# DLRM tower on one core: late transposes and partial sums behind a round of sums, inner products on four quarters of the array

## The reference, cut to what matters

```
e = stack([tbl_f[ids[:, f]] for f in range(40)], axis=1)      # (512, 40, 64)
i, j = np.triu_indices(40, k=1)                               # 780 pairs
z[b, p] = sum_de  e[b, i_p, d] * W[p, d, e'] * e[b, j_p, e']  # (512, 780)
h = relu(concatenate([z, dense_ctx], 1) @ W_top1 + b_top1)    # (512, 796) @ (796, 512)
h = relu(h @ W_top2 + b_top2)                                 # @ (512, 256)
y = h @ W_top3                                                # @ (256, 1)
```

## Time and profile before

| | |
|---|---|
| median of 3 runs | 380.26 us (380.23 to 380.48) |
| the profiled execution, its own time | 379.78 us |
| its span, first to last instruction | 378.0 us |
| PE busy | 348.8 us, 92% |
| DVE busy | 277.1 us, 73% |
| POOL busy | 171.0 us, 45% |
| ACT busy | 45.4 us, 12% |
| mean granted clock of PE | 0.982 of full |

### The profile page before, as it was taken

One profiled execution on the slowest core, in us unless ns is written; L12 is line 12 of the kernel. 1 busy time (PEld: TensorE's weight loads), 2 busy tenths in 40 slices (PEclk: granted clock), 3 DMA queues, 4 the chain that ended last, 5 costly groups with the idle time before them and its releaser, 6 DMA issues.

```text
span 378.0 us, 4628 instructions
## 1 busy us (share of the span) xinstructions
PE 348.8 (92%) x1784; PEld 125.0 (33%) x1784; DVE 277.1 (73%) x287; ACT 45.4 (12%) x73; POOL 171.0 (45%) x261
## 2 busy tenths in 40 slices
PE   0864886899999999999999999999999999999997
PEld 0532332433333333333333333333333333333342
DVE  3999998569687777866758877796778788878420
ACT  2112310111010030101010120000000000300142
POOL 6888888506788775544535553252344100000000
PEclk9978898999999999999999999999999999999999
DMA  5355632012162421121122112220221000000000
GB/s 186 90 167 163 180 125 62 14 57 69 30 264 76 134 74 28 58 69 33 46 71 69 45 37 66 69 69 10 65 68 59 10 2 0 2 1 0 2 0 0
DMA packets 11448, 24.29 MB, mean 64 GB/s; under 512 B 3857, under 2 KB 3857, under 8 KB 11298
## 3 DMA queue, kind: packets, MB, share of 16 engines
q1 hardware_dynamic: 7330, 19.79, 15.6%
q0 software_dynamic: 4096, 4.20, 5.4%
HBM read 23.98 MB, written 0.00 MB: 63 GB/s over the span
## 4 chain that ended last, share of the span: by engine, by line
PE 86%; DVE 9%; DMA 2%; ACT 1%; issue 1%; SPq 0%
PE y_ps L491 46%; PE z_ps L515 24%; DVE one_hot L392 7%; PE t_ps L470 4%; PE y_ps L523 3%; PE t_ps L446 3%; PE t_ps L461 2%; DMA table<-in_small_tables 2%; PE y_ps L498 2%; PE y_ps L553 2%; DVE x L401 1%; DVE table_parts L386 1%; DVE prod L422 1%; PE t_ps L559 0%; ACT x L326 0%
## 5 line engine op out<-in xcount | busy, mean ns | idle before, releaser
L422 DVE TENSOR_TENSOR prod<-y_ps,x 128x1024 f32<-128x1024 f32 x190 | 220.8, 1218 | 61.6 <-PE y_ps L491 58.6
L491 PE MATMUL y_ps<-x,w_sb 64*128 64x512 f32 x760 | 185.5, 617 | 12.1 <-DVE prod L422 5.1
L302 POOL DMA_INDIRECT rows<-in_tbl,ids_sb x128 | 126.0, 984 | 124.0 <-PE y_ps L491 92.7
L491 PEld LDWEIGHTS y_ps<-x,w_sb 64*128 64x128 f32 x760 | 67.1, 188 | 117.2 <-issue 59.1
L515 PE MATMUL z_ps<-prod,selector 128*32 128x512 f32 x780 | 94.3, 598 | 0.0
L297 POOL MEMSET spacer<- 128x256 f32 x127 | 44.3, 349 | 0.2
L515 PEld LDWEIGHTS z_ps<-prod,selector 128*32 128x32 f32 x780 | 20.4, 109 | 67.0 <-issue 36.3
L392 DVE TENSOR_SCALAR one_hot<-ids_all,numbers 128x512 fp32r<-128x512 int32 x64 | 34.4, 607 | 0.0
L446 PE MATMUL t_ps<-one_hot,table_parts 128*128 128x512 f32 x56 | 18.6, 479 | 14.0 <-DVE one_hot L392 9.7
L328 ACT ACTIVATE x<-t_ps 128x512 f32<-128x512 f32 x15 | 9.0, 599 | 156.4 <-PE t_ps L461 151.4
L446 PEld LDWEIGHTS t_ps<-one_hot,table_parts 128*128 128x128 f32 x56 | 11.9, 226 | 21.6 <-issue 12.7
(11 more groups left out here) (36 smaller groups left out, 59.8 us busy)
## 6 DMA issues: line engine op xcount, KB each, us to landing
w_sb<-in_w_units SPq DMA_DIRECT2D x25, 512.0 KB
ids_all<-in_ids_one_hot SPq DMA_DIRECT2D x8, 256.0 KB
table<-in_small_tables SPq DMA_DIRECT2D x8, 256.0 KB
rows<-in_tbl,ids_sb POOLq DMA_INDIRECT x128
w_sb<-in_w SPq DMA_DIRECT2D x1, 1792.0 KB
w_sb<-in_w SPq DMA_DIRECT2D x1, 512.0 KB
ids_sb<-in_ids SPq DMA_DIRECT2D x1, 80.0 KB, 2.0
z_sb<-in_dense_t SPq DMA_DIRECT2D x1, 32.0 KB
```

What stands on the lines that cost most here:

```text
L302: pool.indirect_dma_start(rows[:, n % ROW_SLOTS, bt, h * D:(h + 1) * D], None, tables[f], bass.IndirectOffsetOnAxis(ap=ids_sb[:, bt, f:f + ...
L422: dve.tensor_tensor(prod[:, at:at + 2, :], y_ps[:, s % Y_SLOTS], leaf, ALU.mult).then_inc(prod_ready, 1)
L491: ins = pe.matmul(y_ps[:, slot, h, :], w_sb[own, c % W_SLOTS, at:at + P], x[own, m, :], start=True, stop=True)
```

## The change

Three things are edited. In `plan_jobs`, the turn of every pair from k = 7 on is moved to the nearest earlier place behind a round of sums, 0 to 3 units earlier. The partial sums of the first layer are put 8 units apart in place of 6, so that all of them stand behind a round. And the inner units are laid out anew: before, the two fields' matmuls went from rows 0 to 63 into partitions 64 to 127 and from rows 64 to 127 into partitions 0 to 63, two on each of two quarters of the array; now the four matmuls go to four different quarters. The weights, the copies of the "mix" job and the rows of `W_top1` are laid out to match. The rows are split between banks so that bank 0 gets low to low and high to high, and bank 1 gets low to high and high to low.

```diff
-PARTIAL_EVERY = 6
+PARTIAL_EVERY = 8
@@ pairs_of
-    return [(1 - n % 2, n // 2, n % 2, 2 * (a + n) + 1 - n % 2, 2 * (a + n) + n % 2) for n in range(4)]
+    return [(n % 2, n // 2, n % 2 ^ n // 2, 2 * (a + n) + n % 2, 2 * (a + n) + 1 - n % 2) for n in range(4)]
@@ plan_jobs
         at = FIRST[k] - LEADS.get(k, LEAD)
+        if k > max(ONE_HOT_PAIRS):
+
+            at -= (at - SUM_LAG - ROUND) % ROUND
@@ ACT, mix
-                    k, own = 4 * q + n, slice(D * (n % 2), D * (n % 2) + D)
+
+                    k, into, other = 4 * q + n, D * (n % 2 ^ n // 2), D * (1 - n % 2)
                     wait_x(act, k)
-                    act.activation(x_mix[own, q % MIX_SLOTS, n // 2, :], x[own, k, :],
+                    act.activation(x_mix[into:into + D, q % MIX_SLOTS, n // 2, :], x[other:other + D, k, :],
                                    ACT.Copy).then_inc(mixed, 1)
@@ PE, multiply, inner unit
-                for own, into, first in ((low, high, 1), (high, low, 0)):
-                    for bank in range(2):
-                        k = 4 * unit[1] + 2 * bank + first
-                        ins = pe.matmul(y_ps[into, slot, bank, :],
-                                        w_sb[own, c % W_SLOTS, at + D * bank:at + D * bank + D], x[own, k, :],
-                                        start=True, stop=True)
+                for bank in range(2):
+                    for h, own in enumerate((low, high)):
+                        ins = pe.matmul(y_ps[(low, high)[h ^ bank], slot, bank, :],
+                                        w_sb[own, c % W_SLOTS, at + D * bank:at + D * bank + D],
+                                        x[own, 4 * unit[1] + 2 * bank + h, :], start=True, stop=True)
```

## The result

The changed kernel takes 375.86 us (median of 4 runs, 375.31 to 376.20) against 380.28 us for the kernel before in the same runs: ratio 0.9879, 95% interval 0.9864 to 0.9894. That is 4.4 us less, and 0.3 us above the forecast of 375.6 us. The profiled execution took 376.20 us, the slowest of the four, with a span of 374.4 us.

What follows compares the result with a forecast made beforehand. PE was taken to bound the kernel from 75 to 354 us, DVE keeping pace. -2.73 - 3.44 + 1.52 = -4.65 us, giving 375.6 us, range 374.7 to 377.4.

Steps and rivals of the forecast that it cites:

- 13 cuts: Past 75 us, moved turns and partial sums no longer cut pieces of units: 13 times 0.21, 2.73 us less.
- 4 inner units: Units 28, 63, 114 and 181 on four quarters take two steps, not four: 0.86 us each, 3.44 us less.
- 2 waits for ACT: At units 135 and 151 a partial sum waits for ACT's copy of the turn: 0.76 us each, 1.52 more.
- The first inner unit: At 50.05 us, off the bound stretch: its gain is nothing, since PE then waits 3.94 us for DVE anyway.
- The mix copies: ACT's copies in the mix job: new partitions cost nothing, and even a copy twice as long would stay hidden.
- The Trainium skill's rule against it: Different row tiles can't work on one PSUM bank together: inner units would stay at four steps, bringing 0.
- The lower bound: Turn and partial sum share shape 128*128, so perhaps 0.20 us for changing shape goes: each wait 0.56 us.
- the wait's cover: Behind the waiting partial sum stand only the round's own units; DVE, whose work waits for them, has 24% idle.
- cover (a): DVE catches up in each round; a late product cost 0.31 us in 1 of 31 runs of four units.
- sign of being wrong: The forecast would be wrong if PE's idle time ahead of a fourth unit grew.
- DVE becomes the bound: Rival, 5%: inside rounds, each of 13 newly whole rounds loses 0.31 us, 4.0 in all; 379.6 us, no change.
- 2.0 us to landing: Gathers' landing time, taken from the load of the ids; at turn 11, the tightest, 2.8 us would remain.

Runs made afterwards that it cites:

- the jobs alone: Changed `plan_jobs` with the inner units left on two quarters as in the kernel before; 379.37 us, ratio 0.9980 to the kernel before.
- quarters alone: Inner units on four quarters as in the change, jobs left where they were in the kernel before; 376.38 us, ratio 0.9898.
- no neighbours: Changed kernel with turns 17 and 18 a round earlier, so no turn and partial sum are adjacent; 373.86 us, ratio 0.9839.

## Why the prediction was right

The forecast was 375.6 us and 375.86 came. The late stretches, and the chains in them, settle each term of the sum:

| term | predicted | measured | from |
|---|---|---|---|
| 13 cuts | -2.73 | -2.60 | pieces of the chain, 0.20 each; 2.63 by the jobs alone (0.80 + 1.52 + 0.31) |
| 4 inner units | -3.44 | -3.41 | quarters alone |
| 2 waits for ACT | +1.52 | +1.52 | change less no neighbours |
| late product at unit 119 | not in the sum | +0.31 | 3.94 less 3.63 in the chain |
| sum | -4.65 | -4.20 | late stretch; the terms give -4.18 |

**The cuts** were right in place and number, and 0.01 us each too dear: 1.06 + 2.78 and 3.63 are rounded, and the chains drift apart by 0.20 with each cut. **The quarters** were the step that no row showed, and the full factor came: two steps in place of four, 1.02 us against the 1.01 predicted. The first inner unit was put at nothing, since DVE decides when PE goes on at 59 us. The chains agree: in the changed kernel too a product of DVE (57.96) stands ahead of that piece (59.15). With the unit back on two quarters the median is 375.99 us against 375.86, which can't tell a gain below 0.3 us from none. The mix copies were put at nothing as well, though two of the four of each unit now go from one half of the partitions to the other. They take 628 ns each, against 627 before.

The Trainium skill's rule against it ("TensorEngine Tiling (Array Packing)", PSUM Pressure) would have given 1.87 us for an inner unit of this layout, where low to low and high to high write bank 0 at the same time; the trace disagrees: the unit takes 1.02 us, and with each half of the rows in a bank of its own it is 1.02 as well. The two quarters here write different partitions of the bank. What happens on the same partitions isn't tried.

**The waits** were right in size: 0.60 + 0.02 + 0.61 + 0.04 + 1.98 = 3.25 in the chain against 0.59 + 1.91 = 2.50 for the two apart. That is 0.75 for each wait, against the 0.76 predicted. The lower bound, by which the change of shape would go between a turn and a partial sum, did not come in: the partial sum takes 1.98 behind the wait, no less than elsewhere. And what was said of the wait's cover held too: DVE does not use the pause, and nothing comes back when it is taken away.

**The late product** is the term that the sum lacked. The prediction named a late product (one run in 31, cover (a)) and gave such products 0.3 to 0.6 in the spread, but not in the sum. This one was no chance, and the trace of before could have told: the same product was late there, and the cut behind unit 120 hid it. The timeline of before (see the 1.22 of idle time ahead of it) and of after:

```profile
239.40 2.36 DVE L422 TENSOR_TENSOR prod<-y_ps,x 128x1024 f32<-128x1024 f32 x2 [1.22 <-PE y_ps L491]
```

```profile
236.65 4.61 DVE L426 TENSOR_TENSOR prod<-y_ps,x 128x1024 f32<-128x1024 f32 x4 [1.81 <-PE y_ps L495]
```

In both the first product starts 1.5 us behind the start of its run in the chain (237.87 before, 235.12 after). In the kernel before the run was two units and then turn 16, so the product had time; in the whole run the fourth unit waits for it. The prediction's sign of being wrong, more idle time of PE ahead of a fourth unit, did come, at one run. The rival "DVE becomes the bound" came true in its loss at this one round. The 13 cuts make only 10 newly whole rounds: two rounds had two cuts each (77 and 78, 153 and 154), and that of inner unit 63 stays in pieces. The rival's 4.0 us should thus have been 3.1. Its reason was another one too: DVE was not behind with its work here, since it had 1.81 us of idle time ahead of the late product.

**The early part.** In the profiled execution of the change the units at 59 to 66 us ran longer at half clock than in that of before, and that took 0.63 us of the gain there (59.15 to 66.61 is 7.46 us, against 59.77 to 65.98, 6.21 us, less 0.62 us by which it started earlier). That -4.20 + 0.63 = -3.57 is the profile's difference (374.4 - 378.0 = -3.6). In the medians there is no such loss: they differ by 4.42 us, 0.22 more than the late stretch. So part of the closeness to 375.6 is luck. The terms as measured give 380.26 - 4.20 = 376.1, and the early part, which varies by more than this from one execution to the next, brought 0.2 of it back. The kernel before has mean clocks of 0.968 to 0.982 as well in later runs. What decides how long the half clock lasts stays open; that it is the first inner unit's length isn't supported.

**The gathers.** No turn waits for one: every turn in the late stretch of the changed kernel takes 0.59 or 0.60 us. The prediction's 2.0 us to landing was taken from another kind of transfer, though. In the changed kernel the gathers issued from 118 to 126 us landed 3.7 us after their issue (the last number), where the prediction had 0.95 + 2.0:

```profile
rows<-in_tbl,ids_sb POOLq DMA_INDIRECT x6, 3.7
```

## What to carry to other kernels

When one engine's row of work sets the end, sum the pieces of the chain: a piece's cost and the cost of each change between shapes are there, and here cuts, new overlaps, new waits and one late product added up to within 0.02 us of the 4.20 measured. A cut that costs 0.2 us can be hiding a lateness of another engine; before taking it out, look whether a product behind it was late in the trace of before. And when jobs are lined up on common places, look for two that now stand next to each other and share a buffer: spreading them again gave 1.5 us more.

## What the runs showed of the hardware that was not expected

DVE starts a product 0.3 us late at places 128 of its instructions apart: at units 55 and 119, and with 32 instructions more at 39 and 103. With four more the first two places fall on products that DVE starts straight behind another, and nothing is lost on the chain.

The cause could be the loading of DVE's code. The page of the profile of before has two instruction queues:

```profile
q8 instruction: 14, 0.23, 0.3%
q14 instruction: 8, 0.07, 0.1%
```

The 14 packets of q8 with 0.23 MB together are some 16 KB each, the eight of q14 with 0.07 MB some 8 to 9 KB. A packet of q14 follows each late product and moves with it: it starts 1.6 to 2.0 us behind the product. The transfers from 139.8 to 140.8 us before (late product at 138.24), from 115.9 to 116.9 with 32 more (114.83), and from 133.5 to 134.5 with four more (at unit 53), in this order:

```profile
q14 instruction: 1, 0.01, 3.0%
```

```profile
q14 instruction: 1, 0.01, 2.2%
```

```profile
q14 instruction: 1, 0.01, 1.9%
```

Other packets of q14, such as one at 140 to 142 us in all three, stay where they are. That ties the place to the loading of instructions. Why the product is late ahead of the packet is not shown. The Trainium skill ("Advanced Engine Details and Errata", ISA Cache) says that an engine's instructions are held in lines of 16 KB, 256 instructions each, only two of them, and that the size can be set for each engine. By the 16 KB the distance would be 256, an estimate from that page. The runs show half of it for DVE, and packets of half that size on q14.

PE runs float32 matmuls on all four quarters of the array at once (64 rows by 64 columns each, 512 columns of moving data) in 1.02 us, which is two steps of 0.43 us and 0.16 us on top, with results in two banks, also where quarters with different rows write one bank. Two quarters at a time took 1.87 us for the same work.
